# Sums of squares of q by eight products with 128x128 weights a pair in place of sixteen with 128x64

## What is computed

```python
q = l2norm(q) * DK ** -0.5          # l2norm(x) = x * rsqrt(sum(x*x, -1) + EPS)
k = l2norm(k)
def step(Sstate, xs):               # scan over the 256 positions
    q_t, k_t, v_t, g_t, b_t = xs
    Sstate = Sstate * exp(g_t)
    kv = einsum('bhk,bhkv->bhv', k_t, Sstate)
    delta = (v_t - kv) * b_t
    Sstate = Sstate + k_t[..., None] * delta[..., None, :]
    return Sstate, einsum('bhk,bhkv->bhv', q_t, Sstate)
...
var = mean(o * o, -1)
o = o * rsqrt(var + EPS) * norm_weight * sigmoid(z)
```

## Time and profile before

| | |
|---|---|
| median of 3 executions | 885.0 us (876.76 to 885.98) |
| the profiled execution, its own time | 881.22 us |
| its span | 879.4 us |
| mean granted TensorE clock | 0.981 |
| TensorE, products busy | 802.5 us |
| TensorE, weight loads busy | 548.9 us |
| VectorE busy | 705.0 us |
| ScalarE, GpSimd busy | 324.9 us, 277.7 us |

### The profile page before, as it was taken

The page is one execution under the profiler, slowest core; times in us unless marked ns, Lnnn a source line. Parts: engine busy times, 40 slices in busy tenths (PEclk is TensorE's granted clock), DMA queues, the critical chain, the costliest instruction groups (busy, mean ns, idle before and its releaser), DMA issues.

```text
span 879.4 us, 29218 instructions
## 1 busy us (share of the span) xinstructions
PE 802.5 (91%) x12586; PEld 548.9 (62%) x12586; DVE 705.0 (80%) x1224; ACT 324.9 (37%) x737; POOL 277.7 (32%) x186
## 2 busy tenths in 40 slices
PE   1699999988999999999999999999998989989885
PEld 1345566666766666766766676666665766676664
DVE  4899988885888989797988889898979777976533
ACT  3245432432515334443435143434443343432110
POOL 3052305134161605133241615142534406070101
PEclk9999999999999999999999999999999999999898
DMA  8141411404031313213231314124051303110201
GB/s 239 34 95 18 129 24 21 102 19 99 11 70 39 79 39 64 67 23 64 58 70 34 79 39 91 40 45 91 13 103 23 81 10 69 26 32 15 37 3 48
DMA packets 129151, 49.34 MB, mean 56 GB/s; under 512 B 110976, under 2 KB 120576, under 8 KB 128896
## 3 DMA queue, kind: packets, MB, share of 16 engines
q1 hardware_dynamic: 128400, 47.34, 24.8%
q10 hardware_dynamic: 624, 0.15, 0.1%
HBM read 39.85 MB, written 7.60 MB: 54 GB/s over the span
## 4 chain that ended last, share of the span: by engine, by line
PE 66%; DVE 18%; DMA 4%; issue 4%; SPq 3%; ACT 2%; POOL 1%; POOLq 0%; DVEq 0%; ACTq 0%
PE bank L664 19%; DVE kq L250 6%; PE bank L727 5%; PE bank L685 5%; PE bank L845 5%; PE bank L815 3%; PE bank L785 3%; PE bank L755 3%; PE bank L769 3%; PE bank L796 3%; PE bank L750 3%; PE bank L692 2%; PE bank L759 2%; PE bank L757 2%; PE bank L818 2%
## 5 line engine op out<-in xcount | busy, mean ns | idle before, releaser
L664 PE MATMUL bank<-xnT,wq 128*128 128x512 f32 x512 | 251.0, 615 | 6.9 <-DVE kq L250 6.9
L250 DVE SCALAR_TENSOR_TENSOR kq<-bank,cw,kq 128x510 f32<-128x510 f32 (+2 forms) x288 | 214.5, 745 | 15.5 <-ACT kq L951 8.1
L1126 POOL TENSOR_TENSOR Sd<-St,dec 128x256 f32<-128x256 f32 x32 | 23.5, 734 | 370.3 <-DVE St L369 287.3
L664 PEld LDWEIGHTS bank<-xnT,wq 128*128 128x128 f32 x512 | 89.9, 192 | 80.4 <-issue 68.0
L1120 POOL TENSOR_TENSOR kqg<-kq,rows 128x1024 f32<-128x1024 f32 x32 | 77.3, 2422 | 112.0 <-issue 59.8
L951 ACT ACTIVATE kq<-bank,cw 128x512 f32<-128x512 f32 x96 | 65.8, 685 | 116.8 <-PE bank L664 52.5
L1130 POOL TENSOR_TENSOR ost<-ost,cst 128x8 f32<-128x8 f32 x32 | 53.5, 1673 | 65.8 <-DVE ost L381 64.9
L815 PE MATMUL bank<-d,ATP 64*64 64x64 f32 x1024 | 69.1, 234 | 3.5 <-ACT d L1013 1.9
L845 PE MATMUL bank<-wo,oT 128*128 128x256 f32 x256 | 70.8, 395 | 0.8 <-DVE oT L393 0.8
L727 PE MATMUL bank<-kq 64*64 64x128 f32 x1024 | 69.1, 274 | 0.9 <-DVE kq L250 0.5
L815 PEld LDWEIGHTS bank<-d,ATP 64*64 64x64 f32 x1024 | 57.1, 140 | 15.4 <-ACT d L1013 10.2
(11 more groups left out here) (132 smaller groups left out, 1314.2 us busy)
## 6 DMA issues: line engine op xcount, KB each, us to landing
rows<-decay_rows SPq DMA_DIRECT2D x64, 256.0 KB, 4.9
wq<-wqkvz_dram SPq DMA_DIRECT2D x16, 512.0 KB
inverse_blocks<-UU SPq DMA_DIRECT2D x16, 256.0 KB, 2.0
wguT<-wgu_dram SPq DMA_DIRECT2D x8, 256.0 KB, 3.3
woraw<-wout_dram SPq DMA_DIRECT2D x16, 128.0 KB, 2.6
base_blocks<-ATP SPq DMA_DIRECT2D x128, 16.0 KB, 1.8
UU<-base_blocks SPq DMA_DIRECT2D x16, 128.0 KB
U<-inverse_blocks SPq DMA_DIRECT2D x128, 16.0 KB, 2.0
```

The costliest lines, as they stand in the source:

```text
L250: nc.vector.scalar_tensor_tensor(out=y[:, :, t:S], in0=p[:, :, 0:S - t], scalar=cw[:, m, i // 2, 3 - t:4 - t], in1=y[:, :, t:S], op0=ALU.m ...
L664: last = nc.tensor.matmul(ring[i % 2][:], wq[:, q, kc, i // 2, :], xnT[:, kc, (i % 2) * 512:(i % 2) * 512 + 512], start=kc == 0, stop=kc = ...
```

## The change

The sixteen products of a pair, each with one unit's 64 columns as weights, become eight, each with 128 columns, which are two neighbouring chunks of one sequence. A product now fills all 128 partitions of the bank at once: chunk 2t the lower half, chunk 2t + 1 the upper. The results stand in the same places as before. The waits in front, the signal behind and the place in TensorE's order are the same, and no other engine's instructions change.

```diff
                     pe.wait_ge(sqq_done, m + 1)
                     pe.wait_ge(vt_done, m * 8 + 8)
-                    for u in range(UNITS):
-                        last = nc.tensor.matmul(TR[hs[u % 2], u - u % 2:u - u % 2 + 2], kq[:, 1, u // NCH, u % NCH * C:u % NCH * C + C], k("hsel"), start=True, stop=True)
+                    for b in range(B):
+                        for t in range(2):
+                            last = nc.tensor.matmul(TR[:, b * NCH + 2 * t:b * NCH + 2 * t + 2], kq[:, 1, b, t * P:t * P + P], k("hsel"), start=True, stop=True)
                     last.then_inc(qst_done, 1)
```

## The result

The changed kernel took 898.83 us (median of 4 executions, 892.07 to 901.69) against 885.49 us (median of 4). The ratio is 1.0177, 95% interval 1.0127 to 1.0227: slower by 15.6 us of 883. The two medians are 13.3 us apart: a ratio is worked out from the single executions, those more than 1.5% above the fastest of their kernel left out, and is not the quotient of the medians. The forecast was 892 us, +8.8. The profiled execution is the fastest of the four: 892.07 us, span 890.3, 10.9 us above that of before.

What follows compares the result with a forecast made beforehand. TensorE, running one hand-written order, was taken as the bound. Eleven pairs on the chain add 8.07 us and five off it 0.69, so 883.1 + 8.8 gives 892 us, range 884 to 899.

Steps and rivals of the forecast that it cites:

- The bound and the mechanism: TensorE's fixed order bounds the run; weight loads pace the q-square-sum group, which grows from 1.03 to 1.86 us.
- the tail: Time after the group's load slots before the next group can load: 0.13 us, unchanged by the edit.
- (a): A 128-column load costs no more than a 64-column one: -0.4 us, no change; chance 0.08.
- (b): The number of instructions is the price, 28 ns a load: -6 us, faster; chance 0.05.
- The saved shape changes: Where a neighbouring group is 128*128, the change of array shape goes away: 1.1 us saved over the pairs.
- the way in: 128*128 group in front: first load hidden and 0.09 us of gap gone, 0.20 us saved a pair.
- the way out: 128*128 group behind: the 0.13 us before the next group's loads is saved.
- The cover off the chain: Pairs 1, 2, 4, 5 and 12, where waits hide the longer group: 0.69 us comes through, at most 3.69.
- the sum: 8.07 us from eleven pairs on the chain plus 0.69 us from the five off it: +8.8 us.
- (c): The group is longer but TensorE's waits for VectorE and ScalarE behind it shrink: +3 us; chance 0.11.
- (d): TensorE's clock falls to half in a quarter of the pairs, 4 x 1.7 us more: +15.6 us; chance 0.04.

Runs made afterwards that it cites:

- one half after the other: Kernel before with its sixteen 128x64 products reordered, first the eight of the array's lower half, then the eight of the upper: ratio 1.0176, median 893.87 us.
- the two later series: The changed kernel run twice more without edit, against the kernel before: ratios 1.0208 (median 896.78 us) and 1.0149 (median 898.07 us).
- quarters: Kernel before with 32 products a pair of 128x32 weights, by turns in the four quarters of the array's columns: ratio 1.0058, median 883.28 us.

## Why the prediction was wrong in size

**The bound and the mechanism held.** TensorE was the bound and the loads set the group's pace. A load of 128 columns holds the array for 0.112 us (forecast 0.108), one of 64 columns for 0.058 (forecast 0.056), and the tail is then 0.10 us, not 0.13; the small errors cancel: the group went from 1.03 to 1.88 us (forecast 1.86), and one half after the other shows directly that the old speed was two halves side by side. Rivals (a) and (b), a full load as cheap as a half one and the number of instructions as the price, are out.

**The saved shape changes held.** Five groups behind a 128*128 group take 1.68 us on the chain, 0.20 less, as forecast for the way in. On the way out, in pairs 2 and 15, the next group loads 1.78 us after the first of this one, 0.10 less (forecast 0.13).

**The cover off the chain: right in sum, by pieces that the runs don't separate.** I gave pairs 1, 2 and 12 nothing, pair 4 a cost of 0.05 and pair 5 one of 0.64. After the change TensorE's chain passes all sixteen groups, so the cover was thin and is used up: behind the group of pair 4 VectorE's tap now waits 1.25 us for ScalarE, where it took the data up 0.78 us late before:

```profile
277.77 0.69 ACT L952 ACTIVATE kq<-bank,cw 128x512 f32<-128x512 f32 x1 [3.22 <-PE bank L719]
278.56 1.53 DVE L250 SCALAR_TENSOR_TENSOR kq<-bank,cw,kq 128x510 f32<-128x510 f32 x2 [1.25 <-ACT kq L952]
```

TensorE's later wait for the gated output is still there, 1.2 us ( 1.1). The whole of the length is the last column of the table of clocks: 8.1 and 10.0 us for the changed kernel, where the sum was 8.8. Rival (c), more cover than that, is out.

**The step that failed** is the clock, rival (d): I gave it a chance of 0.04 and put it at nothing in the sum. I argued that half clock shows behind idle time, that the array is loaded without a pause here, and that streams of small products elsewhere ran at 1.00. Here PE and PEld read as busy, and the clock falls right behind the group in about one pair of five, ten of 48. In the means the changed kernel has 13 to 19 us more at half clock than the kernel before, 5 to 7 us of time. With the rest they make 17.1 and 15.6 us between the mean spans of the two later series (by their ratios 18.4 and 13.2).

What I had written for rival (d), four stretches at 1.7 us and 898.7 us in all, met the 898.83 by luck: a stretch of 3.4 us costs 1.3 us (0.39 for each microsecond), not 1.7, and the time at half clock is that of four to six such stretches. In the three profiles the stretches behind groups come to 11 us a profile on average, and those profiles have 10 us more at half clock than the one of the kernel before. The other executions ran longer at half clock still; that this too stands behind the groups is likely, but no trace shows it. Why the clock falls in some pairs and not in others stays open.

The Trainium skill, TensorE: Matmul & The Clock Gate, section HAM oscillation, has the clock fall in idle gaps of TensorE. Here it also falls where PE is at 1.00 and PEld at 0.93 and 0.98 in the two microseconds before (pair 8 above). With equal loads it fell behind ten of 48 groups of two-column products and behind none of 48 with 48 or 96 columns. The same skill's TensorEngine Tiling, Key Properties, that tiles load in parallel, is borne out by the group's 1.75 us against 1.03.

## What to carry to other kernels

A group of products with few columns is paid by its weight loads: count the columns that have to be loaded and how many column tiles load side by side, not the instructions. Fewer, wider weights are a loss once they take parallel loading away; a neighbour that uses the whole array gave back only 0.2 us on the way in and 0.1 on the way out, of 0.85. Where such a group gets long, look at the granted clock in the microseconds behind it, and not only behind idle time; if it falls, let the products stream more columns under the loads, which here took 4.5 and 7.3 us off. Read the clocks of all executions and not only of the profiled one: a shorter group alone did not keep the clock up (quarters).

## What the runs showed of the hardware that I had not expected

- The granted clock fell to half, with PE shown busy 1.00 all the while, behind 12 of 64 groups of 1.75 to 1.88 us of weight loads with two-column products, and behind none of 48 whose products stream 48 or 96 columns under the same loads.
- One float32 load holds its part of the array for 0.112 us at 128 columns, 0.058 at 64 and 0.032 at 32, and two halves or four quarters load side by side: the same 2048 columns of weights take 1.88, 1.03 and 0.64 us.
